# A gated cross-attention and expert kernel: the first rotated q pair summed on VectorE, two weight remainders on GpSimd, and some of the opening's order changed

## The reference, cut to what matters

```python
x = x + tanh(g_xattn) * attention(layernorm(x), ctx, ctx, wq, wk, wv, wo)
#   q, k = rope(layernorm(x) @ wq.T), rope(ctx @ wk.T);  v = ctx @ wv.T
#   scores over the last 65 keys (j <= i, j >= i - 64), softmax, @ v, @ wo.T
x = x + tanh(g_ffn) * ffn(layernorm(x))
#   shared experts: gelu(x @ up.T) @ down.T
#   routed: softmax(x @ router.T), the 4 highest of 16 as gates on each expert's gelu
```

## Time and profile before

| what | value |
|---|---|
| median of 3 runs | 516.3 us (516.02 to 517.77) |
| profiled execution, its own time | 516.1 us |
| its span | 514.3 us |
| TensorE busy | 502.7 us (98%) |
| VectorE, ScalarE, GpSimd busy | 359.8, 314.8, 253.9 us |
| GpSimd busy, 30 to 40 and 40 to 50 us | 9.58 and 9.84 us |
| TensorE busy, 40 to 50 us; granted clock | 7.08 us; 0.95 |
| granted clock, 50 to 60 us | 0.87 |

### The profile page before, as it was taken

The page is one execution under the profiler, slowest core; times in us unless marked ns, Lnnn a source line. Parts: engine busy times, 40 slices in busy tenths (PEclk is TensorE's granted clock), DMA queues, the critical chain, the costliest instruction groups (busy, mean ns, idle before and its releaser), DMA issues.

```text
span 514.3 us, 12328 instructions
## 1 busy us (share of the span) xinstructions
PE 502.7 (98%) x4394; PEld 423.9 (82%) x4394; DVE 359.8 (70%) x1171; ACT 314.8 (61%) x869; POOL 253.9 (49%) x198
## 2 busy tenths in 40 slices
PE   8997999999999999999999999999999999999997
PEld 5787899889989988988888888877887887788885
DVE  6888856758675687766978576796668665855454
ACT  5496686566756657765776783875545545644442
POOL 4999899779887978987997620001000100000000
PEclk9999999999999999999999999999999999999999
DMA  7452215011031101201220128415811581166021
GB/s 263 118 180 64 78 38 160 2 37 39 17 104 38 39 1 38 61 20 39 78 57 24 38 90 303 102 21 144 271 19 22 138 281 14 26 162 224 1 33 48
DMA packets 47723, 44.12 MB, mean 86 GB/s; under 512 B 29168, under 2 KB 31472, under 8 KB 47664
## 3 DMA queue, kind: packets, MB, share of 16 engines
q1 hardware_dynamic: 47664, 43.35, 29.7%
HBM read 30.62 MB, written 2.23 MB: 64 GB/s over the span
## 4 chain that ended last, share of the span: by engine, by line
PE 86%; DVE 6%; issue 2%; POOL 2%; ACT 2%; DMA 1%; SPq 0%; DVEq 0%; POOLq 0%; ACTq 0%
PE ring L1030 60%; PE psS L1030 10%; PE psO L1233 5%; PE psS L1202 5%; PE psT L1214 4%; DVE wl L856 2%; DVE arena L783 1%; DVE arena L926 1%; DMA raw<-in_w 1%; POOL arena L467 1%; POOL arena L469 1%; ACT prob L632 1%; DVE arena L780 1%; DVE oTl L940 1%; PE psT L1165 1%
## 5 line engine op out<-in xcount | busy, mean ns | idle before, releaser
L1030 PE MATMUL ring<-xTh,wh 128*128 128x512 f32 x268 | 107.9, 403 | 0.2 <-DVE lex L798 0.2
L1030 PE MATMUL ring<-xTh,wl 128*128 128x512 f32 x268 | 105.2, 393 | 0.0
L1030 PE MATMUL ring<-xTl,wh 128*128 128x512 f32 x268 | 105.1, 392 | 0.0
L473 POOL TENSOR_TENSOR prob<-prob,rinv 128x512 f32<-128x512 f32 x62 | 66.9, 1079 | 16.4 <-DVE rinv L936 16.4
L565 ACT ACTIVATE oTh<-prob 128x512 fp32r<-128x512 f32 x64 | 40.4, 631 | 54.3 <-PE ring L1030 25.9
L839 DVE TENSOR_TENSOR oTl<-prob,oTh 128x512 fp32r<-128x512 f32 x64 | 44.0, 687 | 35.6 <-ACT oTh L565 35.1
L549 ACT ACTIVATE sneg<-ring 128x512 f32<-128x512 f32 x72 | 42.8, 595 | 33.5 <-PE ring L1030 33.4
L492 POOL TENSOR_TENSOR rstd<-vare,mhalf 128x4 f32<-128x4 f32 x8 | 9.7, 1213 | 104.1 <-DVE vare L750 104.1
L1030 PEld LDWEIGHTS ring<-xTh,wh 128*128 128x128 f32 x268 | 50.3, 188 | 12.1 <-issue 0.6
L831 DVE TENSOR_TENSOR prob<-sneg,arena 128x512 f32<-128x512 f32 x64 | 44.1, 690 | 22.3 <-ACT sneg L549 22.3
L648 ACT ACTIVATE pT<-psT 128x512 f32<-128x512 f32 x64 | 38.0, 594 | 35.3 <-PE psT L1214 35.3
(11 more groups left out here) (132 smaller groups left out, 1236.0 us busy)
## 6 DMA issues: line engine op xcount, KB each, us to landing
arena<-gate_scratch SPq DMA_DIRECT2D x64, 256.0 KB, 6.3
raw<-in_e SPq DMA_DIRECT2D x18, 256.0 KB, 2.7
raw<-in_w SPq DMA_DIRECT2D x16, 256.0 KB, 3.4
arena<-arena SPq DMA_DIRECT2D x16, 256.0 KB, 3.1
arena<-arena SPq DMA_DIRECT2D x16, 192.0 KB, 3.4
pT<-pT SPq DMA_DIRECT2D x96, 32.0 KB, 2.0
out<-x SPq DMA_DIRECT2D x16, 128.0 KB, 6.1
x<-in_x SPq DMA_DIRECT2D x3, 512.0 KB, 4.5
```

The source lines that it names most:

```text
L473: pool.tensor_tensor(prob[:, c % BUFS, :, :], prob[:, c % BUFS, :, :], rinv[:, c % BUFS, :].unsqueeze(2).to_broadcast([P, TT, P]), ALU.mul ...
L1030: last = pe.matmul(out, a, b, start=start and i == 0 and j == 0, stop=stop and i == n - 1 and j == 2, skip_group_check=check)
```

## The change

GpSimd takes the weight remainders 4 and 5 (q1 and v1) from VectorE. VectorE makes the sin product and the sum for the first q pair of unit 0 itself (`join_first`), and both pairs of k of unit 1 are rotated behind the first two score maxima. On GpSimd pair 0 of q of unit 1 stands ahead of pair 1 of its k. Piece 9 is rounded on ScalarE ahead of the copy of head 1 and its remainder made on VectorE ahead of the maxima of head 4; piece 10 is rounded on ScalarE in the opening, and its remainder made in step 6 behind the attention remainder, where it stood in step 5. Piece 10's load keeps its place among SyncE's, at the end of the opening. TensorE's order is as it was.

```diff
--- before.py
+++ after.py
@@ -46,12 +46,12 @@
 ORDER = [("k", 0), ("v", 0), ("q", 0), ("k", 1), ("q", 1), ("v", 1), ("q", 2), ("k", 2), ("v", 2), ("y", 0),
          ("q", 3), ("k", 3), ("v", 3), ("y", 1), ("y", 2), ("y", 3)]
 PIECE_OF = {name: i for i, name in enumerate(ORDER)}
-LO_ON_P = (2, 6, 12, 13, 14, 15)
+LO_ON_P = (2, 4, 5, 6, 12, 13, 14, 15)
 DIVIDED_ON_A = 2
 SPLIT_Q = 3
 OPENED = 5
 CLOSING = 61
-WEIGHT_STEPS = {5: 10, 6: 11, 7: 12, 8: 13, 11: 14, 12: 15, 41: 16, 45: 17, 49: 18, 51: 19, 53: 20, 55: 21}
+WEIGHT_STEPS = {6: 11, 7: 12, 8: 13, 11: 14, 12: 15, 41: 16, 45: 17, 49: 18, 51: 19, 53: 20, 55: 21}
 PRELOADED = 4
 
 
@@ -421,7 +421,7 @@
                     store(n)
 
             for job in [("w", 0), ("w", 1), ("w", 2), ("w", 3), ("v", 0), ("w", 4), ("w", 5), ("w", 6),
-                        ("q", 0), ("v", 1), ("w", 7), ("w", 8), ("w", 9)]:
+                        ("q", 0), ("v", 1), ("w", 7), ("w", 8), ("w", 9), ("w", 10)]:
                 do(job)
             for c, jobs in steps:
                 for job in jobs:
@@ -497,12 +497,13 @@
             pool.wait_ge(in_sin, 16)
             rotate_pair(1, 0, 0)
             rotate_pair(1, 0, 1)
-            rotate_pair(0, 0, 0)
+            do(("w", 4))
+            do(("w", 5))
             rotate_pair(0, 0, 1)
             do(("w", 6))
             rotate_pair(1, 1, 0)
+            rotate_pair(0, 1, 0)
             rotate_pair(1, 1, 1)
-            rotate_pair(0, 1, 0)
             divide(2)
             rotate_pair(0, 1, 1)
             divide(3)
@@ -668,9 +669,10 @@
             do(("v", 1))
             copy_transposed(0)
             softmax_numerator(2)
+            do(("w", 9))
             copy_transposed(1)
             softmax_numerator(3)
-            do(("w", 9))
+            do(("w", 10))
             round_att(0)
             softmax_numerator(4)
             for c, jobs in steps:
@@ -783,6 +785,15 @@
                     dve.tensor_tensor(dst[:, pairs, :], part,
                                       cos[:, :].unsqueeze(1).to_broadcast(part.shape),
                                       ALU.mult).then_inc(qk_mul[i], 1)
+
+            def join_first():
+
+                part, dst = swap[:, 0, 0, :], qT[:, 0, 0, :]
+                dve.wait_ge(in_sin, 16)
+                dve.wait_ge(qk_swap[0], 1)
+                link(dve.tensor_tensor(part, part, sin[:, :], ALU.mult))
+                dve.wait_ge(qk_mul[0], 1)
+                dve.tensor_tensor(dst, dst, part, ALU.add).then_inc(qk_rot[0], 1)
 
             def router(b):
                 dve.wait_ge(r_pe, b + 1)
@@ -951,12 +962,11 @@
             do(("xT", 0))
             do(("w", 3))
             rotate(("q", 0), 0)
-            do(("w", 4))
+            join_first()
             rotate(("q", 0), 1)
-            do(("w", 5))
-            rotate(("k", 1), 0)
             score_max(0)
             score_max(1)
+            rotate(("k", 1), 0)
             rotate(("k", 1), 1)
             invert(0)
             rotate(("q", 1), 0)
@@ -967,14 +977,14 @@
             do(("w", 7))
             do(("w", 8))
             invert(2)
+            do(("w", 9))
+            score_max(4)
             invert(3)
-            score_max(4)
             score_max(5)
             rest_att(0)
             rotate(("q", 2), 0)
             invert(4)
             rotate(("q", 2), 1)
-            do(("w", 9))
             for c, jobs in steps:
                 if c == G + 3:
                     dve.wait_ge(rw_hi, 1)
@@ -987,6 +997,8 @@
                     invert(c - 1)
                 if c in attended:
                     rest_att(attended[c])
+                if c == OPENED + 1:
+                    do(("w", 10))
                 for job in jobs:
                     if (c, job[0]) == (CLOSING - 2, "xT"):
                         invert(CLOSING - 2)
```

## The result

| | before | changed |
|---|---|---|
| median | 516.27 us | 513.85 us |
| ratio, 95% interval | | 0.9946 (0.9934 to 0.9959) |
| profiled execution, span | 516.1, 514.3 us | 513.85, 512.1 us |
| granted clock over the span | 0.996 | 1.000 |

A forecast was written before the change was run, and what follows sets the result against it. TensorE bounds the kernel, with 6.2 us of loss in its opening. It gets 3.2 us ahead, GpSimd's chain takes back 0.7 us by head 13, leaving -2.5 us: median 513.8 us, range 512.9 to 515.3 us.

The forecast's parts named there:

- The price of a turn: Two-input VectorE operations wait for GpSimd's running operation, then take 0.6 us; GpSimd's next one lasts some 0.45 us longer.
- rival 2: Opening: the join loses its turns to GpSimd's two remainders and the chain loses 1.0 us; 514.8 us, chance 0.08.
- The first join: Unit 0's first q pair on VectorE: first scores 1.1 us earlier, half given back at the values of unit 1.
- q1/0 ahead of k1/1: GpSimd's order in the opening: the 0.70 us wait at heads 4 and 5 goes, their scores start 1.2 us earlier.
- w9 in the hole: Remainder w9 in VectorE's pause before the inversion: oTl ready at about 44.0 instead of 47.8, y starts 3.1 us earlier.
- What is late next: Transposes behind y wait 1.0 to 1.5 us for head 5's division; TensorE stands 3.2 us ahead there.
- The give-back at head 13: GpSimd's chain, full up to head 13's division, allows only 2.5 us, so 0.7 of the 3.2 us is given back.
- The clock: First y: TensorE's clock falls behind the 2.92 us wait, which costs 1.4 us; the change was to keep it up.
- Rival 1: TensorE's clock falls after all in the new wait at 47.8 to 49; 514.6 us, chance 0.08.
- Rival 3: No gain: GpSimd's 2.4 us of pauses stay and TensorE waits at 88.6 as before; 516.2 us, chance 0.10.
- Rival 4: Slower: piece 9 lands late and holds ScalarE and VectorE; 519.3 us for a landing at 37.5, chance 0.04.
- Rival 5: More gain: TensorE keeps its 3.2 us because a turn or two in GpSimd's chain drops out; 513.1 us, chance 0.10.

The follow-up runs named there:

- e7: The changed kernel with weight remainders 12 and 14 on VectorE instead of GpSimd; 514.69 us.
- e3: The kernel before with only q1's first pair ahead of k1's second pair on GpSimd; 516.37 us against 516.33 us.
- e12: The kernel before with only w9 moved, w10 in its old place, and head 4's maxima ahead of head 3's inversion; 514.12 us against 516.37 us.
- e5: The changed kernel with one extra 128x512 GpSimd sum ahead of head 13's division; 514.78 us.
- e6: The changed kernel with the same extra GpSimd sum one head later, behind head 14's division; 514.19 us.
- e9: The changed kernel with head 5's division ahead of the first pair of unit 2's k on GpSimd; 513.64 us.
- e1: The kernel before with only w9 and w10 moved, and head 4's maxima ahead of head 3's inversion; 513.90 us against 516.33 us.
- e4: The kernel before with the join and the order of q1 and k1, without the moves of w9 and w10; 516.08 us against 516.33 us.
- e10: The changed kernel with e9's order and also remainder 12 on VectorE; 513.14 us.
- e2: The kernel before with only the join on VectorE, remainders 4 and 5 on GpSimd, k1's first pair behind the score maxima; 515.77 us against 516.33 us.

## Why the prediction was right, point by point

**What bounds the kernel.** Right: the 6.2 us of waits and low clock in TensorE's opening were not all to be had. 3.4 us came to TensorE and 3.1 us stayed (from the common start). One reading was incomplete: the kernel before has a third wait for GpSimd, 1.3 us for L447 at the very start, which the change leaves as it is.

**The price of a turn.** Right in kind and size, and it has a second face that e7 showed: the wait of VectorE is as long as the rest of GpSimd's operation, so what it costs depends on which operation it meets (0.69, 1.68 and 2.47 us for the same kind of remainder). The Trainium skill (SBUF — State Buffer, section "SBUF: two separate sides") has the port pair that VectorE and GpSimd share held for a whole instruction. The 2.47 us beside a 2.40 us operation agree. VectorE kept out by two GpSimd operations in a row, which rival 2 drew from it, stands in none of the rows shown.

**The first join.** Right: no wait at the first scores, and the values of unit 1 are held by VectorE's product for k1 (a wait of 0.23 us). From the common start the first scores are 1.3 us earlier (12.13 against 13.44 us) and the values of unit 1 0.9 us (17.58 against 18.45), where 1.1 and 0.5 us were forecast: a third was given back and not half.

**q1/0 ahead of k1/1.** The wait went, as said, and from the common start the scores are 1.65 us earlier (24.28 against 25.93 us), where 1.2 us was forecast. e3 shows that alone the order reaches nothing, since VectorE's late oTl still sets y.

**w9 in the hole.** Right, and by the medians it is nearly the whole change (e12, together with the exchange of head 4's maxima and head 3's inversion). y was forecast at 44.8 and came at 45.16, or 0.45 us early by the common start. The stretched division of head 2 (1.49 us at 33.96) came as said, with a wait of 0.72 us.

**What is late next.** Right: 1.45 us of wait for head 5's division, forecast 1.0 to 1.5 us. From the common start the division ends at 49.67 - 0.81 = 48.86, where 48.8 was forecast, or 49.25 if w11 fell ahead of it. w11 did fall on the chain (GpSimd's sum beside it took 1.61 us at 47.06), but GpSimd made up for it elsewhere; the wait is long because y came 0.45 us earlier than forecast.

**The give-back at head 13.** The place and the cause are right (e5, e6, e9); the size was off. Forecast were -3.2 us falling to -2.5 us; measured -3.4 us falling to -3.1 us. The term at fault is the length of the chain: 2.5 us shorter in the sum, 71.26 - 68.30 = 2.96 us in the traces. The two rows, before and changed, have the stretch, its length and each engine's busy time, GpSimd's ahead of the last three figures:

```profile
17.34:88.60 71.26, 66.47 (x771) 58.52 (x769) 55.01 (x215) 50.68 (x174) 67.43 (x52) 0.98 0.36 102
```

```profile
18.04:86.34 68.30, 65.60 (x771) 56.95 (x770) 55.74 (x215) 50.91 (x174) 67.12 (x52) 1.00 0.37 108
```

Of these 2.96 us, GpSimd's busy time gives 0.3 us (67.43 to 67.12 us; I had 0.1 us) and its idle time 2.65 us (3.83 to 1.18 us; I had 2.4 us from a list that leaves out the smallest gaps).

**The clock.** The step had the fall as certain before. It is not: 9 of 29 executions of the kernel before in the comparison with e1 to e4, and 22 of 70 in all comparisons with e1 to e12, went without it. Executions at 0.995 to 0.997 are 0.7 us longer than those at the full clock (516.39 against 515.70 us), and not by the 1.4 us that TensorE loses in y. That the missing slack at head 13 hides the other half would fit theory 1, but there is no trace of the kernel before at the full clock to show it. Against its executions at the full clock the change is worth 515.7 - 513.85 = 1.85 us; the rest of the 2.4 us goes with the falls that no longer occur.

**The hit is in part luck.** 513.8 us came from -2.5 us on one execution whose start was early by 0.8 us and whose clock fell. The chain shortened by 0.45 us more than forecast and the changed kernel's profiled execution started 0.8 us later. The two starts lie near the two ends of what the traces show (7.44 to 8.36 us), so 0.8 us of the span's difference is chance; how the starts are spread in the executions that have no trace stays open.

**Rivals.** Rival 1 (a fall in the new wait) did not occur in the changed kernel. Rival 2 is seen in the traces of e5 and e6, at 0.4 us. Rival 3 is refuted by GpSimd's list of waits. Rival 4: piece 9 was there in time; ScalarE rounded it from 32.01 without a wait, and VectorE's w9 began at 32.87 as its turn came. Rival 5's mechanism (a shorter chain) is what e10 builds on purpose.

## What to carry to other kernels

Before removing a wait of the engine that bounds the kernel, follow the next engine to the first place where it has no slack, and add up its pauses up to there: here that sum (2.4 us in the list, 2.65 us of idle time that closed) and not the 6.2 us of loss was about what was won. A move that fills a hole of a nearly full engine (w9 here) can by itself bring nearly all that several others bring together, and is worth testing alone; the parts need not add up. Moving work to a neighbour with a shared resource is only free if it doesn't land beside that neighbour's longest operation.

## What the runs showed of the hardware that I had not expected

- TensorE's clock falls behind a wait in some executions of a kernel and not in others: in 20 of 29 of the kernel before, whose trace has a wait of 2.92 us, and in 8 of 12 of e4, whose trace has 2.03 us and no fall. e2's trace has a fall at a wait of 2.65 us (0.41 us a matmul behind it). An execution's granted clock over the span then has one of two values, 0.995 to 0.997 or 0.993, and the kernel before is about 0.7 or 2.1 us longer than at the full clock; where the clock fell in the executions without a trace is not shown.
- A two-input VectorE operation of 0.68 us lasted 2.47 us beside one 2.40 us GpSimd operation.
- The start of the first key product, behind the load of the context, moved between 7.44 and 8.36 us over the traces. What lies behind head 13's transposes is 425.6 to 425.8 us in all 13 of them.
